# Joining the four layers and the five stages after them into one block of a Perceiver-like kernel

## What is computed

```python
x = x + _L0_xattn_ref(_layernorm(x), ctx, ids, ...)      # 4 layers: self attention, cross attention, gated ffn
x = x + _L0_attn_ref(_layernorm(x), u, v)                # messages from 16 rank-64 factors
x = x + _L0_ffn_ref(_layernorm(x), weight, disha)        # a linear map and a pooled one
x = x + _L1_xattn_ref(ctx, _layernorm(x), mask, ...)     # 64 latents attend to 1601 context rows each
x = x + _L1_attn_ref(_layernorm(x), w_qkv, w_out)        # causal self attention
x = x + _L1_ffn_ref(_layernorm(x), gate_w, ..., w2, b2)  # 8 experts, top 2 of each token
```

## Time and profile before

| what | value |
|---|---|
| median of 3 runs | 509.67 us (509.57 to 510.04) |
| the profiled execution | 507.16 us, span 505.0 us |
| mean granted clock of PE | 0.986 |
| PE busy | 463.1 us, 92% of the span, 5430 products |
| PEld busy | 400.6 us, 79% |
| DVE busy | 360.1 us, 71% |
| ACT busy | 267.4 us, 53% |
| POOL busy | 227.3 us, 45% |
| DMA | 27.07 MB, mean 54 GB/s |

### The profile page before, as it was taken

How to read it: one execution, slowest core, us unless ns; L and a number is a source line. 1 busy time by engine, 2 the same in 40 slices (tenths; PEclk the granted TensorE clock), 3 DMA queues, 4 the chain that set the end, 5 groups by cost and what they waited for, 6 DMA issues and landing times. The chain is left out here.

```text
span 505.0 us, 14335 instructions
## 1 busy us (share of the span) xinstructions
PE 463.1 (92%) x5430; PEld 400.6 (79%) x5430; DVE 360.1 (71%) x1028; ACT 267.4 (53%) x714; POOL 227.3 (45%) x342
## 2 busy tenths in 40 slices
PE   0899999999999999939899898999999999899997
PEld 0777896788778876929898787888888988689997
DVE  4286668566856685547788778998899987584644
ACT  3367756775777577613334455655555564432221
POOL 1393149315821682133599431749889511220000
PEclk9899999999999999969999999999999999999999
DMA  7800120102019000012202431040220000000000
GB/s 221 298 3 2 38 70 17 32 11 83 3 42 388 11 3 2 1 51 94 69 3 70 137 126 65 2 132 1 67 68 1 2 2 1 1 2 1 12 0 12
DMA packets 10031, 27.07 MB, mean 54 GB/s; under 512 B 1425, under 2 KB 4838, under 8 KB 9702
## 3 DMA queue, kind: packets, MB, share of 16 engines
q1 hardware_dynamic: 9958, 26.09, 15.4%
HBM read 25.82 MB, written 0.26 MB: 52 GB/s over the span
## 5 line engine op out<-in xcount | busy, mean ns | idle before, releaser
L893 POOL TENSOR_TENSOR rstd<-ss,par 128x1 f32<-128x1 f32 x52 | 28.6, 551 | 103.0 <-ACT sq L729 103.0
L749 ACT ACTIVATE pr<-sd 128x512 f32<-128x512 f32 x56 | 34.6, 627 | 6.0 <-DVE sd L802 5.6
L1264 POOL TENSOR_TENSOR xh<-xh,rsx 128x512 f32<-128x512 f32 (+1 forms) x32 | 29.8, 930 | 4.6
L1781 POOL TENSOR_TENSOR rstd<-mv,par 128x1 f32<-128x1 f32 x21 | 5.3, 250 | 57.6 <-DVE mv L1616 48.0
L1260 POOL TENSOR_TENSOR xh<-cx,mvx 128x512 f32<-128x512 f32 (+1 forms) x32 | 30.8, 962 | 0.7
L733 ACT ACTIVATE h<-y,rstd 128x128 f32<-128x128 f32 x48 | 19.2, 400 | 9.8 <-POOL rstd L893 9.3
L1239 DVE BATCH_NORM_STATS2 stx<-cx 128x6 f32<-128x128 f32 x104 | 22.7, 275 | 0.7 <-DMA cx<-ctx_in 0.7
L887 POOL TENSOR_TENSOR kblk<-qk,cf 128x512 f32<-128x512 f32 x20 | 20.9, 1043 | 0.9
L879 POOL TENSOR_TENSOR qk<-rope 128x256 f32<-128x256 f32 x20 | 14.5, 726 | 13.7 <-DVE rope L786 13.6
L1249 POOL TENSOR_TENSOR rsx<-rsx,par 128x13 f32<-128x13 f32 x8 | 20.1, 2516 | 0.6
L729 ACT ACTIVATE sq<-y 128x129 f32<-128x129 f32 x52 | 15.9, 307 | 8.4 <-DVE y L833 6.7
(11 more groups left out here) (566 smaller groups left out, 1522.8 us busy)
## 6 DMA issues: line engine op xcount, KB each, us to landing
cx<-ctx_in SPq DMA_DIRECT2D x13, 768.0 KB
we<-we_in SPq DMA_DIRECT2D x8, 514.0 KB, 8.7
wc<-wc_in SPq DMA_DIRECT2D x4, 768.5 KB, 5.9
wa<-wa_in SPq DMA_DIRECT2D x5, 387.0 KB, 3.0
wb<-wb_in SPq DMA_DIRECT2D x4, 256.5 KB, 4.1
uvT<-uvT_in SPq DMA_DIRECT2D x1, 1024.0 KB, 4.8
uv<-uv_in SPq DMA_DIRECT2D x1, 1024.0 KB, 6.8
cx<-ctx_in SPq DMA_DIRECT2D x13, 32.5 KB
```

The lines of the kernel that those rows point to most:

```text
L749: nc.scalar.activation(pr[:, t, at:at + 512], sd[:, t, at:at + 512], ACT.Exp).then_inc(s[piece], 1)
L893: nc.gpsimd.tensor_tensor(rstd[:, t:t + 1], ss[:, t:t + 1], par[:, 1:2], ALU.pow).then_inc(s[piece], 1)
L1264: nc.gpsimd.tensor_tensor(part, part, rsx[:, b, tiles].unsqueeze(2).to_broadcast(shape), ALU.mult).then_inc(xm["c_normed"], 1)
```

## The change

The layers' block is gone: its fast and general paths stand at the head of the one block that all engines run, each followed by the later stages. `FAST` and `LAST` are joined in one list for each engine; `JOINT.first` is the place behind the last layer piece, and `opening` issues all up to it on the fast path. One pool of banks serves both. z_moments, z_power and z_norm are in the layers' queue for all four tiles. New waits keep the reused buffers apart. All due times are new. The tables cut to the entries that the text speaks of, the core of the rest:

```diff
-PERIOD, SKEW = 94.96, (0.0, 6.64, 13.36, 19.85)
+PERIOD, SKEW = 95.43, (0.0, 6.74, 13.36, 19.85)
-    "PE": {"memory": -64.59, ... "down": 70.36},
-    "ACT": {... "mem_k": -49.09, ...},
-    "DVE": {... "gated": 64.05, "hidden": 67.21, "y3": 74.17},
-    "POOL": {"pow1": -32.40, "rope_sum": -19.02, ... "kc": 0.12, ...},
+    "PE": {"memory": -56.61, ... "down": 80.98},
+    "ACT": {... "mem_k": -52.70, ...},
+    "DVE": {... "gated": 72.90, "hidden": 78.17, "y3": 81.04},
+    "POOL": {"pow1": -24.86, "rope_sum": -9.86, ... "kc": -35.17, ...},
...
-FINAL = {"PE": {}, "ACT": {"square_f": 233.37}, "DVE": {"norm_f": 235.66, "x_f": 248.65, "z_moments": 253.29, "z_norm": 346.43},
-         "POOL": {"pow_f": 468.90, "z_power": 528.02}}
+FINAL = {"PE": {}, "ACT": {"square_f": 0.18}, "DVE": {"norm_f": 4.73, "x_f": 6.55, "z_moments": 10.88, "z_norm": 17.41},
+         "POOL": {"pow_f": -7.85, "z_power": 0.96}}
...
+        "ZED": (0.00, 660771.82, 1299974.23, 1299977.23)}
...
-    "PE": {"z_turn": -163.01, "across0": -85.18, "across1": -97.75, ...
+    "PE": {"z_turn": -1299965.84, "across0": 2.39, "across1": 0.00, ...
-    "ACT": {"z_turned": -160.93, "uT0": -75.86, ...
+    "ACT": {"z_turned": -1517092.93, "uT0": 0.40, ...
-    "DVE": {"z_moments": -191.77, "z_norm": -168.26, "uT1": -78.52, ...
+    "DVE": {"uT1": 5.51, "un1": 19.30, ...
-    "POOL": {"z_power": -216.21, ... "c_normed": (65.56, 72.39, 84.79, 85.41), ...
+    "POOL": {... "c_normed": (-110283.05, -110274.31, -110263.52, -110261.20), ...
...
+JOIN = 2141178.39
+
+class Joint:
+    def __init__(self):
+        self.queue = {e: sorted([(w, 0, l, t, p) for w, l, t, p in FAST.queue[e]] + [(JOIN + w, 1, i, g, p) for w, i, g, p in LAST.queue[e]])
+                      for e in AT}
+        self.first = {e: 1 + max(n for n, z in enumerate(q) if z[1] == 0) for e, q in self.queue.items()}
+        FAST.bank, LAST.bank = {}, {}
...
-        unat = [sd[:, 2:4, :], pts[:, 2:4, :]]
-        th = pr[:, 0:2, :]
-        qh = pr[:, 2:4, :].rearrange("p w (a j q) -> p w a j q", a=2, q=L)
+        unat = [pts[:, 2:4, :], sd[:, 2:4, :]]
+        th = [pr[:, 2 * i:2 * i + 2, :] for i in range(2)]
+        qh = [a.rearrange("p w (a j q) -> p w a j q", a=2, q=L) for a in th]
...
         def x_sp(sp):
+            sp.wait_ge(am["z_moments"], T)
             sp.dma_start(xw[:], xw_in).then_inc(xw_loaded, 16)
...
-                    sp.wait_ge(xm["c_moments" if kind == "stats" else "c_center"], 4 * k + 4)
+                    sp.wait_ge(xm["c_moments" if kind == "stats" else "c_normed"], 4 * k + 4)
...
             elif piece == "un0":
+                if i < 2:
+                    act.wait_ge(s["y3" if i else "y2"], one(LAYERS - 1, T - 1))
...
             elif piece in ("th0", "th1"):
-                x_wait(act, "qh" + piece[2], i)
+                if i < 2:
+                    act.wait_ge(s["y3"], one(LAYERS - 1, 2 * i + 1))
+                x_wait(act, "v%d" % (1 - int(piece[2])), i - 1)
...
             elif piece in ("qh0", "qh1"):
                 k = int(piece[2])
-                x_wait(dve, "v%d" % (1 - k), i)
                 x_wait(dve, "th%d" % k, i + 1)
-                nc.vector.tensor_scalar(pr[:, 2 + k, :], th[:, k, :], 0.5, 0.5, ALU.mult, ALU.add).then_inc(am[piece], 1)
+                nc.vector.tensor_scalar(th[i % 2][:, k, :], th[i % 2][:, k, :], 0.5, 0.5, ALU.mult, ALU.add).then_inc(am[piece], 1)
...
             elif piece == "top_diag":
-                x_wait(dve, "top_row", i + 1)
-                nc.vector.tensor_scalar(dg[i % 2][:], ident, mx1[i % 2][:, 0:1], -1.0, ALU.mult, ALU.mult).then_inc(xm[piece], 1)
+                x_wait(dve, "top_row", 2 * i + 1)
+                nc.vector.tensor_scalar(dg[i % 2][:], ident, mx1[i % 2][:, 0:1], -1.0, ALU.mult, ALU.mult).then_inc(xm["top_row"], 1)
...
+        def opening(eng, piece_of, layer_of, engine):
+            for _, kind, i, j, p in JOINT.queue[engine][:JOINT.first[engine]]:
+                if kind:
+                    piece_of(eng, p, i, j)
+                else:
+                    layer_of(eng, FAST, p, i, j)
+                    if (p, j) == ("k_groups", T - 1):
+                        pool_bias(eng, i + 1)
...
         def x_pool_start(pool):
+            pool.wait_ge(am["z_moments"], T)
...
         with nc.Block() as block:
-            block.sync(x_sp)
...
             @block.tensor
             def _(pe):
+                def whole():
+                    general(pe, pe_piece, "PE", pe_any)
+                    pe.wait_ge(s["y3"], one(LAYERS - 1, T - 1))
+                    ahead(pe, x_pe_piece, "PE")
+
+                either(pe, lambda: opening(pe, x_pe_piece, pe_piece, "PE"), whole)
                 x_queue(pe, x_pe_piece, pe_piece, "PE")
```

More of the change, by code:

```diff
@@ L108, in __init__ @@
     def __init__(self, engines, when):
-        self.queue = {e: sorted((when(p, l, t), l, t, p) for p, layers in pieces for l in layers for t in range(T)
-                                if p[:2] != "z_" or t < T - 1)
+        self.queue = {e: sorted((when(p, l, t), l, t, p) for p, layers in pieces for l in layers for t in range(T))
                       for e, pieces in engines.items()}
@@ L142 @@
 XAHEAD = 3
[L143 to L149, removed]
-YAT = {
[L151 to L163, removed]
-            "c_squares": (-51.45, -46.47, -45.13, -39.74), "c_root": (-41.89, -38.84, -35.89, -32.07),
-            "weights": (-17.57, -15.92, -15.21, -11.80), "sum_taken": -5.51, "u_turned": -0.80, "o_turned": -59.83,
-            "hT1": -32.17, "q_groups": -8.45, "expa": 26.82, "expb": 27.69, "turneda": 34.13, "turnedb": 39.85,
-            "oT": 57.93, "m_turned": 83.08, "route_exp": 16.30, "cho_turned": 48.79, "relu0": 2.20},
-    "DVE": {"z_moments": -191.77, "z_norm": -168.26, "uT1": -78.52, "un1": -67.90, "qh0": -44.21, "qh1": -45.19,
-            "vt0": -34.15, "x_G": -14.40, "f_moments": -12.86, "f_norm": -6.40, "x_F": 0.38, "consts": -10.90,
-            "x_moments": 1.33, "x_norm": 6.81, "l_moments": 11.85, "l_norm": 20.03, "l_sums": 40.98, "q_norm": 50.47,
-            "qk1_taken": 71.66, "l_scaled": 78.77, "c_moments": (-53.76, -50.21, -45.47, -42.57),
-            "c_sums": (-45.96, -41.73, -39.11, -33.24), "c_scaled": (-36.69, -32.31, -31.07, -27.56),
-            "c_top": (-33.20, -27.66, -27.56, -26.63), "top_row": -21.84, "top_diag": -19.54,
-            "shifted": (-16.76, -16.43, -16.32, -15.80), "totals": -2.29, "h_recip": 12.67, "h_bias": 9.33,
-            "h_sum": 15.89, "h_done": 18.99, "x_added": -49.09, "n_moments": -48.44, "n_norm": -38.64, "rope": -27.40,
-            "vblk": -21.23, "maxa": 5.61, "maxb": 6.65, "shifta": 7.98, "shiftb": 15.76, "recip": 45.05, "o": 47.41,
-            "y1": 64.17, "m_moments": 66.82, "m_norm": 73.20, "route1": 12.59, "route2": 35.65, "x_b2": 71.67,
-            "relu1": 0.47, "x_e": 71.79},
-    "POOL": {"z_power": -216.21, "f_power": 13.35, "x_power": 32.28, "x_bias": 77.38, "l_power": 40.98,
-             "l_rnorm": 72.76, "c_normed": (65.56, 72.39, 84.79, 85.41), "c_floor": (-15.75, -9.22, -9.07, -4.12),
-             "n_power": -16.35, "rope_sum": 6.15, "rope_bias": 6.79, "k_groups": 7.96, "m_power": 94.86},
@@ L1842, in _, with fast, whole @@
             def _(pool):
+                pool_bias(pool, 0)
+                def fast():
+                    zero_context(pool)
+                    opening(pool, x_pool_piece, pool_piece, "POOL")
+                def whole():
+                    pool_queue(pool, GENERAL)
+                    pool.wait_ge(s["y3"], one(LAYERS - 1, T - 1))
+                    zero_context(pool)
+                    ahead(pool, x_pool_piece, "POOL")
+                either(pool, fast, whole)
                 x_pool_start(pool)
```

210 lines of the change are left out of this document (133 added, 77 removed).

## The result

The changed kernel takes 505.01 us (median of 20 executions, 502.08 to 510.23), the one before 508.59 in the same session (506.16 to 510.04): 3.6 us less by the medians. The profiled execution took 502.72 for a span of 500.6 (before: 507.16 for 505.0), so the two traces are 4.4 us apart.

A forecast was written before the change was run, and what follows sets the result against it. PE bounds the layers, with a 7.81 us hole behind them from final norms, barrier and jump. Joint -3.1 and reorder -1.5 give -4.6: 502.6 profiled, 505.1 from the 509.67 median; range 500.5 to 508.7.

The forecast's parts named there:

- the joint: Passage from the layers to the later stages, barrier removed: tile 0's v0 claimed 3.1 us earlier in all.
- The layers at nothing, 0.3 either way: In the layers, kc and mem_k come earlier while PE stays full: claimed 0, bounds 0.3 us each way.
- The tail's 0.6: End of the layers: hidden of tile 3 waits on DVE, so the last down ends 0.6 us later, bounds 0 and 1.4.
- Barrier and jump: Between layers and later stages: barrier at most 0.64 us goes, jump over the general path of 2.5 stays; 4.3 us earlier.
- first rival: At the end of the layers the jump costs next to nothing and the clock stays full: -9.2, 500.5; chance 0.18.
- Who is last: After the layers ACT is last ready, across1 starting at 220.8; PE's jump, 217.0 to 219.5, is hidden behind it.
- Step 3: Tile 0's new order after the layers gives 1.2 us back, leaving v0 3.1 us earlier, half clock as before.
- Step 4: Later stages up to the end: new order removes two PE waits, together 1.7 us, of which 1.5 is taken.
- the two named: PE's waits before q_turn of tile 0 (0.64 us) and f_turn of tile 2 (1.09), claimed to come from the old order.
- The even rival: PE's idle time in 270 to 330 grows by 3 to 4.6 us, cancelling the joint's gain: 508.7 to 510.7; chance 0.07.
- The covers named for zero terms: After the layers, SP's loads and POOL's clearing and memsets come earlier, c_moments only after un1: 0, without cover some 1 us.
- The slower rival: Later stages: c_scaled on DVE waits for each sample's last scores, 1.3 us for each of eight: 515.5; chance 0.12.

## Why the prediction was right, and where it was not

The forecast said 505.1, faster by 4.6; measured 505.01, faster by 3.6 to 4.0, and 4.4 between the two traces. What goes and where is right, the sizes are not: the joint was counted at 3.1 and gave 0.96 in the traces, the order behind it at 1.5 and gave 3.44. That these misses cancel is luck, and so is the agreement to 0.1 us, since the kernel before took 508.59 beside the changed one and not the 509.67 that the sum starts from.

- **The layers at nothing, 0.3 either way: too small.** The tail's 0.6 came as worked out (the last down waits 1.07 instead of 0.51). But the layers before it took 0.55 us more: last down at 216.40, not 215.9. The bound was too narrow; that PE is full before and after does not bound 0.3% of its time. (The second trace of the changed kernel has the last down at 217.38; see the last section.)
- **Barrier and jump: right in kind and size.** The jump was taken at 2.5, bounds 0 and 3.1; it is 2.8 by the kernel before without it, 2.63 on PE and 2.28 on ACT. The barrier alone is 0.33, not 0.64. Across1 came 4.06 us earlier, where 4.3 was said. The Trainium skill ("Runtime: NRT & Kernel Launch", Instruction fetch mechanics) says that a taken branch beyond the fetched instructions waits for a fetch, and this trace agrees: 2.63 us, with a packet on an instruction queue at 217.3. The 51 ns that the Trainium skill gives for a branch ("Advanced Engine Details and Errata", Control Flow Timing) do not describe such a jump. The first rival's cause (the jump costs nothing) is refuted, while its price came near: 4.6 us for jump and half clock gave 500.5, and the kernels rid of both take 500.7 and 500.9, the one with a start 1 us sooner and the other with 3.6 us paid at the start, so the agreement is partly chance.
- **Who is last: half right.** "PE's jump hidden behind ACT's" is the wrong way round here: PE is ready at 220.16, ACT's copy waits for it until 220.64, and across1 comes at 221.05 instead of 220.8 because the last down ended 0.5 later. But ACT's jump stands right behind, as the run with PE's removed shows.
- **Step 3, joint 3.1 us earlier: measured 0.96.** Of the 2.1 missing, 0.25 is across1's later start; 0.5 is the half clock, which came as said but held longer (from across1 to z_turn of tile 2 6.3 us, 5.8 counted: the second group took 2.90 us, 2.32 before); and 1.34 is the stop in M0, which no step allowed for although the old trace has one of 1.37 inside M of tile 1 (243.83).
- **Step 4, reorder 1.5: measured 3.44.** 1.0 of it is that old stop, now counted ahead of v0 (1.37 against 0.37 left behind v0). The other 2.4 is PE's waits: the two named went, and so did 1.70 us at 306 for c_turned and 0.63 for f_turn of tile 3, 4.1 in all, while the others grew by 1.7 together. The step was sized at less than half, its cause is right: put back, those places cost 3.46 us of waits.
- **The even rival, the reorder giving back what the joint gains: refuted.** PE idles 4.07 us between 270 and 330, where it idled 6.05.
- **The covers named for zero terms held.** SP's first load for the later stages went out at 220.28 instead of 224.17 and POOL's clearing ended at 225.9; c_moments follows un1 without a wait at 230.32.
- **The slower rival, DVE waiting for the last scores of each sample: refuted.** c_scaled waits for c_root, 1.2 and 0.4 us once each, never for PE.

## What to carry to other kernels

Ask of every branch in a long unrolled program where its far side lies: the path that runs should fall through into what follows, and the jump belongs where the engines wait anyway; several engines that jump together must all be freed before any of it shows. A hole in PE costs its length plus the half clock behind it, here 2.6 us each. And when the order is written out, a few places on an engine that is not the bound can be worth as much as a barrier.

## What was not expected of the hardware

- POOL jumps over its general path too, and nothing shows: its last z_power starts at 220.61 and the memset behind the jump at 221.11. Its general path has no loop, while PE, ACT and DVE have a long one with loops. Whether length decides was not tried.
- PE stops for no visible releaser inside the 64-column products: 1.34, 1.90 and 1.89 behind the same product of M0 in three executions that have the jump and the same order of PE up to there, 1.37 and 1.27 in M of tile 1 with the old order, 3.38 in one kernel without a jump, under 0.7 in all others. The timeline names no releaser, but the DMA record has a candidate for each: the six stops of 1.27 to 3.38 us end 2.3 to 2.9 us after a packet of instruction queue q8 starts (230.1 to 232.48 in the changed kernel, 227.1 to 229.53 in the kernel without a jump), as the jump does (217.3 to 220.16). These look like waits for instructions too, though such packets also come where PE does not stop (224.6 with the general path first). What sets place and length stays open.
- The clock record begins late. In the second trace of the changed kernel it reads 1.00 from 20 to 28 us, but the products say half speed: 2.08 us for the eight of `project` in tile 0, which take 1.16 in the first trace. The first trace then has its half clock in 22 to 26 as a record. The layers up to the last down are 1.06 us longer in the second (197.64 against 196.58), so two executions of one kernel can differ by a microsecond for this alone:

```profile
20.74 2.08 PE L625 MATMUL sm<-hT,wa 128*128 128x128 f32 x8 [0.52 <-ACT hT L761]
```
